# Fetching each tile of edge rows once and copying it on chip to the steps that use it

## The reference, cut to what matters

```python
h = relu(layernorm(x)); x += (segment_sum(h[src], dst) / (deg + eps)) @ W.T + b      # sum
h = relu(layernorm(x)); e = relu(concat(h[src], h[dst]) @ W_edge.T)                   # mlp
x += relu((segment_sum(e, dst) / cnt) @ W_node.T + b)
h = relu(layernorm(x)); x += gat(elu(gat(h)))        # two attention layers of 16 heads
h = relu(layernorm(x)); x += dot_attention(h)        # 2 heads of 64
# gat: e = leaky_relu(al_s[src] + al_d[dst]); a = softmax of e over the edges of dst;
#      out = segment_sum((h @ W)[src] * a, dst)
```

## Time and profile before

| | us |
|---|---|
| median of 3 runs | 6834.45 (6828.22 to 6835.2) |
| profiled execution | 6823.64 |
| its span | 6821.9 |
| busy: PE, weight loads, DVE, ACT, POOL | 3345.8, 2897.9, 2697.0, 2103.5, 3437.8 |
| mean granted TensorE clock | 0.636 |
| DMA: software queue, hardware queue | 289.37 MB, 273.42 MB |

### The profile page before, as it was taken

How to read it: one execution, slowest core, us unless ns; L and a number is a source line. 1 busy time by engine, 2 the same in 40 slices (tenths; PEclk the granted TensorE clock), 3 DMA queues, 4 the chain that set the end, 5 groups by cost and what they waited for, 6 DMA issues and landing times.

```text
span 6821.9 us, 113042 instructions
## 1 busy us (share of the span) xinstructions
PE 3345.8 (49%) x30004; PEld 2897.9 (42%) x30005; DVE 2697.0 (40%) x6412; ACT 2103.5 (31%) x6369; POOL 3437.8 (50%) x3641
## 2 busy tenths in 40 slices
PE   1545445444444454454454534444444555555555
PEld 1434334333333343444444534444444455555454
DVE  4222223211111144444444544444445644444445
ACT  1111112222222233444444434444444322222222
POOL 3666664455555525555555355455454444444443
PEclk9565666767776665556555655555666666666666
DMA  4222222222222222222222232222222333333332
GB/s 114 91 87 88 90 85 83 80 74 78 75 76 77 75 56 75 78 78 82 78 78 82 56 83 81 77 78 81 77 77 62 103 97 100 96 98 96 98 95 80
DMA packets 342830, 564.68 MB, mean 83 GB/s; under 512 B 90413, under 2 KB 160957, under 8 KB 342622
## 3 DMA queue, kind: packets, MB, share of 16 engines
q0 software_dynamic: 124288, 289.37, 16.1%
q1 hardware_dynamic: 218354, 273.42, 12.7%
HBM read 490.31 MB, written 72.84 MB: 83 GB/s over the span
## 4 chain that ended last, share of the span: by engine, by line
another core or an unknown queue 48%; DVE 17%; PE 14%; issue 13%; ACT 3%; DVEq 2%; ACTq 1%; POOL 1%; DMA 0%; SPq 0%; POOLq 0%
PE psA L1564 7%; PE psDS L1189 3%; DVE acc L1683 2%; PE psDS L1542 2%; DVE prod L1589 1%; PE psA L1230 1%; DVE lg L1598 1%; DVE seg L1605 1%; DVE lastmax L1615 1%; DVE lastmax L1613 1%; DVE below L1661 1%; DVE V L1670 1%; DVE prod L1396 1%; DVE lastmax L1617 1%
## 5 line engine op out<-in xcount | busy, mean ns | idle before, releaser
L1165 POOL DMA_INDIRECT GT<-table,srcI x3520 | 3355.5, 953 | 3202.6 <-DVE V L1670 1403.7
L1564 PE MATMUL psA<-V,O 128*128 128x144 f32 (+1 forms) x4176 | 988.6, 425 | 10.8 <-ACT psA L1500 5.5
L1189 PE MATMUL psDS<-nodeQ,Ot 128*128 x2816 | 605.7, 390 | 658.3 <-ACT Ot L1181 559.8
L1564 PEld LDWEIGHTS psA<-V,O 128*128 128x128 f32 x4176 | 918.0, 314 | 17.2 <-issue 11.8
L1189 PEld LDWEIGHTS psDS<-nodeQ,Ot 128*128 128x128 f32 x2816 | 544.6, 290 | 696.4 <-issue 691.3
L1519 PE MATMUL psDS<-stageD,Ot 128*128 128x16 bf16 x4224 | 251.4, 173 | 804.2 <-issue 802.9
L1519 PEld LDWEIGHTS psDS<-stageD,Ot 128*128 128x128 bf16 x4224 | 184.3, 102 | 878.2 <-issue 860.4
L1683 DVE TENSOR_TENSOR acc<-acc,psA 128x1296 f32 (+1 forms) x261 | 381.2, 1460 | 413.8 <-remote 349.8
L1661 DVE TENSOR_TENSOR below<-lg,psDS 128x128 f32<-128x128 f32 (+1 forms) x264 | 62.4, 236 | 1157.8 <-remote 1156.6
L1500 ACT COPY psA<-consts 128x1296 f32<-128x1296 f32 (+1 forms) x261 | 315.0, 1207 | 628.4 <-DVE acc L1683 471.9
L1550 PE MATMUL psDS<-newM,Ot 128*128 128x16 bf16 (+1 forms) x6336 | 256.5, 175 | 430.2 <-issue 291.3
(11 more groups left out here) (244 smaller groups left out, 5286.0 us busy)
## 6 DMA issues: line engine op xcount, KB each, us to landing
Ob<-onehots SPq DMA_DIRECT2D x352, 256.0 KB
Ot<-onehots_turned SPq DMA_DIRECT2D x352, 256.0 KB
GT<-table,srcI POOLq DMA_INDIRECT x3520
onehots<-Ob SPq DMA_DIRECT2D x88, 256.0 KB
onehots_turned<-Ot SPq DMA_DIRECT2D x88, 256.0 KB
first<-first_dram SPq DMA_DIRECT2D x176, 64.0 KB
first_dram<-GT SPq DMA_DIRECT2D x18, 384.0 KB, 5.1
table<-nodeQ SPq DMA_DIRECT2D x40, 128.0 KB, 1.9
```

What stands on the lines that cost most here:

```text
L1165: eng.indirect_dma_start(out=GT[:, p.k, j, 0:table.shape[1]], out_offset=None, in_=table, in_offset=bass.IndirectOffsetOnAxis(ap=srcI[:, p ...
L1189: ins = eng.matmul(psD[:, j, :], Ot32[:, p.q, j, :], at_block(nodeQ, b[j], D), start=True, stop=True)
L1564: ins = eng.matmul(to, O[:, p.q, j, :], V[:, p.q, j, 0:VW], start=False, stop=j == G - 1, skip_group_check=True)
```

## The change

In the first four passes (sum, mlp, gat, gat) GpSimd gathers by tiles, each of the 665 once, in 84 groups of tiles (NT), the last of one tile, into a second ring of 4 × 8 tiles. SP then copies, with one DMA from SBUF to SBUF for each step, the tile of the step into the ring of steps, from which the consumers read as before. Both rings are views of one tensor, `rows_of_edges`; `prod` overlaps its end, for which gat's tile group 3 waits for `parted(0)`.

`copy_rows(p)` waits for the consumer of the step group four back, loads the eight slots of its tiles and two numbers of tile groups into registers, waits for each half until `landed` says that these tile groups are there, issues the DMAs, waits until all have landed, and then counts `copied` up. GpSimd waits for `copied` of the last step group that used the tile group four back, by a register from `tiles_over`. It counts `landed` up for a tile group after the fifth gather of the next one. SP's order in the sum pass is copy of p, then the two stores of p; in mlp and gat the loads of p+1, then the copy of p.

ACT copies the indices of 84 instead of 88 groups in these passes. `srcT` holds indices by tiles; those by steps, which the dot pass needs, are stored to DRAM at the start (`src_steps`, 384 KB) and loaded into `srcT` at the end of SP's work in the second gat pass. The dot pass is as before otherwise. The start has three more loads and seven more small DVE operations, and six more transposes on PE. The mlp pass's node units keep two intermediates in `acc` instead of the unused halves of GT.

```diff
-def sweep(eng, n, turn, early=0, late=0):
+def sweep(eng, n, turn, early=0, late=0, tail=0):
...
-        GT = sb("GT", [P, RING, G, 2 * D])
+        rows_of_edges = sb("rows_of_edges", [P, RING * G * 2 * D + HEADS1 + G * D])
+        flatG = rows_of_edges[:, 0:RING * G * 2 * D]
+        GT = flatG.rearrange("p (r g w) -> p r g w", r=RING, g=G)
+        prod = rows_of_edges[:, RING * G * 2 * D + HEADS1:].rearrange("p (g e) -> p g e", g=G)
+        slots_of_steps = sb("slots_of_steps", [1, SP_], I32)
+        tiles_needed = sb("tiles_needed", [1, NG * 2 + 1], I32)
+        tiles_over = sb("tiles_over", [1, NT - RING], I32)
         consts = sb("consts", [P, 4, 1])
...
+        def by_tiles(w):
+
+            size = RING * G * w
+            return (rows_of_edges[:, 0:size].rearrange("p (r g w) -> p r g w", r=RING, g=G),
+                    rows_of_edges[:, size:2 * size].rearrange("p (n w) -> p n w", w=w))
+
...
-        def loaded(eng, which, table, g, n, most, of=None):
+        def loaded(eng, which, table, g, n, most, of=None, for_waits=False):
             if (eng.engine, which) not in reg_sets:
                 reg_sets[eng.engine, which] = [eng.alloc_register(f"{which}_{j}") for j in range(n)]
             regs = reg_sets[eng.engine, which]
             eng.load(regs, table[0:1, bass.ds(g * (of or n), n)])
+            if for_waits:
+                if (eng.engine, which, "held") not in reg_sets:
+                    reg_sets[eng.engine, which, "held"] = [eng.alloc_register(f"{which}_held_{j}") for j in range(n)]
+                held = reg_sets[eng.engine, which, "held"]
+                for r, to in zip(regs, held):
+                    eng.reg_alu(to, r, 0, ALU.max)
+                regs = held
             return [eng.snap(r, min_val=0, max_val=most) for r in regs]
...
+                eng.wait_ge(tile_zeroed, 1)
+                eng.dma_start(tile_rows[:, 0:WHOLE, :], src[0:WHOLE * P * P].rearrange("(c p e) -> p c e", p=P, e=P))\
+                   .then_inc(load_sem, 16)
+                eng.dma_start(tile_rows[0:MORE, WHOLE, :], src[WHOLE * P * P:E - LEFT].rearrange("(p e) -> p e", e=P))\
+                   .then_inc(load_sem, 16)
+                eng.dma_start(tile_rows[MORE:MORE + 1, WHOLE, 0:LEFT], src[E - LEFT:E].rearrange("(a e) -> a e", a=1))\
                    .then_inc(load_sem, 16)
...
+                eng.memset(tile_rows[:, WHOLE, :], 0).then_inc(tile_zeroed, 1)
...
-                do(eng.tensor_copy, srcT[:, :], psN[:, 0:SC, :].rearrange("p c s -> p (c s)"))
+                do(eng.tensor_copy, tile_rows, psN[:, 0:SC, :])
...
+                do(eng.tensor_scalar, rowi[1][:, 0:NT - RING], firsts_of_tiles, -1.0, None, ALU.add)
+                do(eng.tensor_scalar, tiles_over[:, :], rowi[1][:, 0:NT - RING], G.bit_length() - 1, None, ALU.logical_shift_right)
+                do(eng.tensor_tensor, slots_of_steps[:, :], row[2][:, 0:SP_], row[0][:, 0:SP_], ALU.subtract)
+                do(eng.tensor_scalar, rowi[0][:, 0:SP_], slots_of_steps[:, :], G.bit_length() - 1, None, ALU.logical_shift_right)
+                do(eng.tensor_copy, tiles_needed[:, 0:2 * NG],
+                   rowi[0][:, 0:NG * G].rearrange("p (h j) -> p h j", j=G // 2)[:, :, G // 2 - 1])
+                do(eng.tensor_copy, tiles_needed[:, 2 * NG:2 * NG + 1], rowi[0][:, NG * G - 2:NG * G - 1])
...
+                eng.wait_ge(prepared, marks["src out"])
+                eng.dma_start(src_steps.rearrange("p (c s) -> p c s", c=SC), tile_rows).then_inc(first_stored, 16)
...
-        beside_rows = [[GT[:, r // 2, r % 2 * 4 + 2 * k:r % 2 * 4 + 2 * k + H, D:2 * D] for r in range(SLOTS)] for k in range(2)]
+        own_sums = [acc[:, u * H:(u + 1) * H, 0:D] for u in range(UNITS)]
...
+        def fetch_tiles(eng, table, hold=None):
+
+
+            tables_stored(eng)
+            to = by_tiles(table.shape[1])[1]
+
+            def has_landed(p, many=G):
+                eng.wait_ge(*ring_tiles[p.k](p.i, many - 1))
+                eng.sem_inc(landed.sem, 1)
+
+            def turn(p):
+                is_int = isinstance(p.g, int)
+                if not (is_int and p.g < RING):
+                    eng.wait_ge(*copied(loaded(eng, "over", tiles_over, p.g - RING, 1, NG - 1, for_waits=True)[0]))
+                    apart(eng)
+                if is_int and p.g == RING - 1 and hold is not None:
+                    eng.wait_ge(*hold(0))
+                eng.wait_ge(*index(p.g))
+                apart(eng)
+                many = T - p.g * G if is_int and p.g == NT - 1 else G
+                for j in range(many):
+                    eng.indirect_dma_start(
+                        out=to[:, p.k * G + j, :], out_offset=None, in_=table,
+                        in_offset=bass.IndirectOffsetOnAxis(ap=srcI[:, p.k, j:j + 1], axis=0),
+                    ).then_inc(ring_tiles[p.k].sem, 16)
+                    if j == G // 2 and not (is_int and p.g == 0):
+                        has_landed(p.plus(-1))
+                if many < G:
+                    has_landed(p.plus(-1))
+                    has_landed(p, many)
+            sweep(eng, NT, turn, tail=1)
+
+        def copy_rows(eng, p, w, release):
+
+            to, of = by_tiles(w)
+            last = isinstance(p.g, int) and p.g == NG - 1
+            eng.wait_ge(*release(p.g - RING))
+            apart(eng)
+            at = loaded(eng, "slots", slots_of_steps, p.g, G, RING * G - 1)
+            need = loaded(eng, "need", tiles_needed, p.g, 2, NT - 1, for_waits=True)
+            parts = [(0, G // 2, need[0]), (G // 2, G, need[1])]
+            if last:
+                parts = [(0, G - 1, loaded(eng, "needed_last", tiles_needed, 2 * NG, 1, NT - 1, for_waits=True)[0]), (G - 1, G, NT - 1)]
+            for a, z, group in parts:
+                eng.wait_ge(*landed(group))
+                apart(eng)
+                for j in range(a, z):
+                    eng.dma_start(to[:, p.k, j, :], of[:, bass.ds(at[j], 1), :].rearrange("p o w -> p (o w)"))\
+                       .then_inc(ring_rows[p.k].sem, 16)
+            eng.wait_ge(*ring_rows[p.k](p.i))
+            eng.sem_inc(copied.sem, 1)
+
+        def has_tiles(p):
+
+            return not isinstance(p.g, int) or 0 <= p.g + RING < NT
+
+        def copy_tiles_index(eng, p):
+
+            if not (isinstance(p.i, int) and p.i <= 0):
+                eng.wait_ge(*ring_tiles[p.k](p.i - 1))
+            eng.copy(srcI[:, p.k, :], srcT[:, bass.ds(p.g * G, G)]).then_inc(index.sem, 1)
+
+        def tiles_closed():
+            close((index, landed), NT)
+            copied.close(NG)
...
-                    fetch_groups(eng, NG, table, sums)
+                    fetch_tiles(eng, table)
 
                 @block.sync
                 def _(eng):
                     def turn(p):
+                        copy_rows(eng, p, D, sums)
                         eng.wait_ge(*onehot(p.g))
...
-                        if p.has(RING):
-                            copy_index(eng, p.plus(RING))
+                        if has_tiles(p):
+                            copy_tiles_index(eng, p.plus(RING))
...
-                    fetch_groups(eng, NG, table, prodded)
+                    fetch_tiles(eng, table)
 
                 @block.sync
                 def _(eng):
-                    sweep(eng, NG, lambda p: load_hots(eng, p, (onehot32,), (turned32,)))
+                    def turn(p):
+                        if p.has(1):
+                            load_hots(eng, p.plus(1), (onehot32,), (turned32,))
+                        if p.has(0):
+                            copy_rows(eng, p, D, prodded)
+                    sweep(eng, NG, turn, early=1)
...
-                    fetch_groups(eng, NG, table, values)
+                    if gat:
+                        fetch_tiles(eng, table, parted)
+                    else:
+                        fetch_groups(eng, NG, table, values)
                     phase.gpsimd(eng)
 
                 @block.sync
                 def _(eng):
-                    def turn(p):
+                    def load(p):
                         load_hots(eng, p, (nmax, onehot32), (toedge if gat else turned32, maxedge))
                         eng.wait_ge(*segmax(p.g - RING))
                         apart(eng)
                         eng.dma_start(first[0:HG, p.k, :], first_drams[h][bass.ds(p.g * HG, HG), :])\
                            .then_inc(ring_first[p.k].sem, 16)
-                    sweep(eng, NG, turn)
+
+                    def turn(p):
+                        if p.has(1):
+                            load(p.plus(1))
+                        if p.has(0):
+                            copy_rows(eng, p, VW, values)
+
+                    if gat:
+                        sweep(eng, NG, turn, early=1)
+                    else:
+                        sweep(eng, NG, load)
+                    if to_x == 3:
+                        eng.wait_ge(*index(NT - 1))
```

(30 more changed lines are left out.)

83 lines of the change are left out of this document (50 added, 33 removed).

## The result

The changed kernel takes 7493.13 us (median of 4 runs, 7469.54 to 7495.18) against 6834.49: 1.0958 times the time before, 95% interval 1.0935 to 1.0981. I had forecast 7005 and a range up to 7270. The direction was right; the size was wrong, and with it the price of SP's work and the place of ACT's index copies.

A forecast was written before the change was run, and what follows sets the result against it. Gather bursts were taken as the bound, by their own time and by slowing sequencers. Sum +25, mlp −49, gat +75 twice, starts +41, setup +5 made +172 us, 7006 beside the median; forecast 7005, range 6670 to 7270.

The forecast's parts named there:

- What bounds the kernel before: Gather bursts lie on the path, by their own 1.25 us each and by slowing every sequencer, 7.2 us of each gat group.
- Fewer gathers: −49 us a pass: In the first four passes, 39 fewer gathers at 1.25 us each save 49 us a pass, −196 us in all.
- W: SP's undisturbed work for a group, landing wait included: 7.3 to 8.1 us in sum and mlp, 8.1 to 9.0 in gat.
- Sum pass, I take 12.1: Sum pass: SP's round sets the pace at 12.1 us a group against 11.83 now, +25 us.
- The bound of 13.6: Sum pass: upper end of SP's round, 12.8 to 13.6 us a group if all the slow-down hits an issue.
- The term for the slow-down: On SP, each window of slowed instructions in a gather burst takes 5.5 us, less where it falls into a landing.
- ACT copies the index of fewer groups: 0, it idles: First four passes: ACT's copying of fewer groups' indices changes the time by 0, since ACT idles.
- I take 15.75: Gat passes: 15.75 us a group against 14.9 now, +75 us a pass, with bounds −49 and +185.
- the loop of two groups: Gat: values to onehot32 3.7 us, W, then at most 7.64 to values; 9.7 to 10.2 us a group plus slow-down.
- Pass starts, +41: Heads of the first four passes: group 0's rows come 9.3 to 10.8 us later in each, +41 us.
- setup, +5: Kernel start: the added 384 KB store, three loads and a wait for a memset cost 5 us, bounds 1 and 12.
- rival (b): SP becomes the bound in every pass, crawling over 50 instructions: +548 us, 7380; chance 0.15, shared with one other rival.

## Why the prediction was wrong

- What bounds the kernel before: right for the chips of its runs. Bursts and slowed sequencers make the cycle, and a gather is worth its 1.25 us (275 us for 220, measured). But it isn't "every sequencer": DVE's longest address instruction at L200 is 81 ns where SP's is 1402.
- "Fewer gathers: −49 us a pass": right where nothing else is slower. With two copies of eight, mlp is 52 us below before. In the change mlp lost 21; that its SP round, slowed, is the reason is argued from sum's rows, not shown.
- "W = 7.3 to 8.1 in sum and mlp, 8.1 to 9.0 in gat": the first step that failed. I priced a copy by DMAs of other kinds. Measured free, W is 10.7 in sum and 10.7 to 11.4 in gat. Eight copies take 5.3 to 5.4 where I had 3.3 to 4.1; from the last start to the next store are 1.7, as I had; from the second store in sum to the first copy 2.7, where I had 1.4 for loads and waits. The Trainium skill's rule (Runtime: NRT & Kernel Launch, Instruction fetch mechanics) of some 200 ns a register would have added 0.9 us. The loads of eight and two registers here, 0.53 and 0.48 us, are against it; that section speaks of the loads that the runtime puts around a kernel, and these read SBUF.
- "Sum pass, I take 12.1": it was about 14 for most of the pass, by the same W and the slow-down, then 24 for six groups. The bound of 13.6 was too low for both reasons. The term for the slow-down was too high: a window took 5.5 us from SP in my sum, and the round in a burst is 14.4 against 10.7, 3.7 more. With W right and the 5.5 kept, I would have forecast 16.2; two errors partly cancelled, which is luck.
- "ACT copies the index of fewer groups: 0, it idles": the second step that failed. The wait behind it, which had room in the kernel before, loses it as tile groups fall in number behind the step groups; 121 us in all.
- "I take 15.75" in gat, from the loop of two groups: measured 16.8. I can't claim the loop: moved out of it, the copies gained 15 to 52 us a pass, by what one compares with, where the loop had promised 70 to 110. Without slow-down a round of SP takes 11.35 us and a group of gat 11.4 to 11.7 (1005 and 1027 by 88), so there SP's round is what is shown. With slow-down, my loop with the right W (3.7 + 10.7 + 7.64, by two, and 5.5) gives 16.5; that it comes near 16.8 doesn't show it. Why gat stays 50 to 80 us above before with two copies of eight is not settled. Between values, `copied`, the index and the burst many waits alternate, and no run here took the wait for `copied` away, since that would be a race.
- Pass starts, +41, and setup, +5: 49 and 4 by the windows, the ends of the passes included.
- The chances: my rival (b), SP as the bound in every pass, had 0.15 and ended at 7380. It came nearest, with a W too small and without the index copies: shown in sum, and in gat where nothing is slowed; in mlp it isn't shown. The range ended below it.

## What to carry to other kernels

Price a DMA start, and a queue's wait for its own landing, by rows of just that kind (here SBUF to SBUF), and add up a queue's whole round before giving it a new duty: here 10.7 us against a group of 10.0 to 13. When two rings run at different rates, follow every wait between them to the last group. And time on more than one chip: two pauses of 1.35 us in the gathers of a group were worth 12% on one, and on another even two of 0.7 cost 7%. Before two paused kernels are compared, see whether the pauses are of one length and whether they are the bound.

## What the runs showed of the hardware

Runs of gathers (128 rows each, every 1.25 us) slow the sequencers of PE, ACT and SP to some 0.70 us an instruction on chips where this kernel takes 6830 to 6880 us, and not on the others met, where it takes 4910: there a run of 704 gathers slows nothing, and SP's longest address instruction is 0.30 us. The sequencers of DVE and GpSimd aren't slowed on either. In the changed kernel's trace 213 of DVE's sequencer instructions fall wholly inside a slowed one of SP or ACT, and none takes over 0.11 us. On the slowing chips runs of three with 1.35 us between them bring 810 us, though SP still has instructions of 0.74; runs of four with 2.05 bring 477; and a gap of 0.7 after four brings nothing. What in the chip or its surroundings makes the difference no run shows. The executions of a kernel on one chip agree, so nothing in a single chip's times gives it away; the 0.70 us instructions in SP's rows do.
